# The next round's relative products in steps 0, 1, 2 and 4, and the maximum products spread anew

## The reference

```python
idx = jnp.arange(s)
dist = jnp.clip(idx[None, :] - idx[:, None], -R, R) + R
pe_k = rel_emb_k[dist]
pe_v = rel_emb_v[dist]
...
q = q / jnp.sqrt(jnp.asarray(hd, x.dtype))
score = jnp.einsum('bhqd,bhkd->bhqk', q, k) + jnp.einsum('bhqd,qkd->bhqk', q, pe_k)
attn = jax.nn.softmax(score, axis=-1)
ctx = jnp.einsum('bhqk,bhkd->bhqd', attn, v) + jnp.einsum('bhqk,qkd->bhqd', attn, pe_v)
...
x = x + _L0_attn_ref(_layernorm(x, axis=-1), ...)
x = x + _L0_ffn_ref(_layernorm(x, axis=-1), ...)
```

## Time and profile before

| | |
|---|---|
| median of 3 runs | 2382.93 us (2382.06 to 2384.38) |
| the profiled execution | 2382.3 us, span 2380.6 us |
| mean granted clock of TensorE | 0.981 of full |
| PE busy | 2282.5 us (96%) |
| DVE busy | 1906.6 us (80%) |
| ACT busy | 1429.9 us (60%) |
| POOL busy | 600.4 us (25%) |
| reduces of M, DVE line 1118 | 2048, mean 683 ns |
| exps, ACT line 1085 | 1792, mean 610 ns |

### The profile page before, as it was taken

One profiled execution on the slowest core, in us unless ns is written; L12 is line 12 of the kernel. 1 busy time (PEld: TensorE's weight loads), 2 busy tenths in 40 slices (PEclk: granted clock), 3 DMA queues, 4 the chain that ended last, 5 costly groups with the idle time before them and its releaser, 6 DMA issues. The chain is left out here.

```text
span 2380.6 us, 49031 instructions
## 1 busy us (share of the span) xinstructions
PE 2282.5 (96%) x19244; PEld 1182.6 (50%) x19244; DVE 1906.6 (80%) x3711; ACT 1429.9 (60%) x2720; POOL 600.4 (25%) x355
## 2 busy tenths in 40 slices
PE   7989999999999999999999999999999997999997
PEld 3515544444444444444444454444444444666665
DVE  6777888888888888888888888888888725999996
ACT  3406666666666666666666666666666673444442
POOL 5502222323322222222222222232332220111111
PEclk9959999999999999999999999999999998999999
DMA  5733533332333343433332333333222221111110
GB/s 157 199 88 91 138 85 93 94 95 83 92 92 92 97 110 96 108 99 96 92 93 84 99 98 85 92 97 92 83 83 84 76 77 43 45 44 44 47 50 20
DMA packets 275667, 210.43 MB, mean 88 GB/s; under 512 B 17058, under 2 KB 266628, under 8 KB 275332
## 3 DMA queue, kind: packets, MB, share of 16 engines
q1 hardware_dynamic: 274308, 203.37, 30.9%
q0 software_dynamic: 1152, 4.19, 0.6%
HBM read 113.35 MB, written 93.34 MB: 87 GB/s over the span
## 5 line engine op out<-in xcount | busy, mean ns | idle before, releaser
L1118 DVE TENSOR_REDUCE amax<-psA 128x1 f32<-128x512 f32 x2048 | 1300.5, 683 | 274.2 <-PE psA L828 270.1
L1085 ACT ACTIVATE probs<-psS 128x512 f32<-128x512 f32 x1792 | 927.3, 610 | 378.9 <-PE psS L936 378.9
L828 PE MATMUL psA<-keys,queries 96*128 96x512 bf16 x2048 | 772.0, 390 | 3.1 <-DVE amax L1118 1.9
L936 PE MATMUL psS<-queries,keys 102*128 102x512 bf16 (+7 forms) x2176 | 604.2, 342 | 0.1
L850 PE MATMUL psC<-probs,vals 128*32 128x512 f32 (+7 forms) x4352 | 475.0, 524 | 0.5 <-ACT probs L1085 0.5
L786 POOL TENSOR_TENSOR band_probs<-band_probs,side 128x2048 f32<-128x2048 f32 x64 | 288.9, 4534 | 515.6 <-PE psC L948 515.6
L828 PEld LDWEIGHTS psA<-keys,queries 96*128 96x128 bf16 x2048 | 195.3, 97 | 319.8 <-DVE amax L1118 179.3
L936 PEld LDWEIGHTS psS<-queries,keys 102*128 102x128 bf16 (+1 forms) x2176 | 205.9, 98 | 184.4 <-ACT rel_scores L1064 29.9
L1080 ACT ACTIVATE band_probs<-psS 128x512 f32<-128x512 f32 x256 | 153.0, 598 | 152.2 <-PE psS L925 152.0
L850 PEld LDWEIGHTS psC<-probs,vals 128*32 128x32 f32 (+1 forms) x4352 | 89.1, 102 | 193.8 <-ACT probs L1085 137.5
L1442 PE MATMUL psG<-w_gate_up_T,f_xqT 128*128 128x352 f32 x512 | 160.4, 467 | 0.9 <-ACT f_xqT L1496 0.9
(11 more groups left out here) (161 smaller groups left out, 2014.3 us busy)
## 6 DMA issues: line engine op xcount, KB each, us to landing
rel_skew<-rel_scores SPq DMA_DIRECT2D x32, 2048.0 KB, 7.5
rel_near<-rel_skew SPq DMA_DIRECT2D x64, 1024.0 KB, 8.2
keys<-k_ring SPq DMA_DIRECT2D x48, 256.0 KB, 5.8
queries<-q_parts SPq DMA_DIRECT2D x192, 64.0 KB, 2.4
ctx_d<-rden SPq DMA_DIRECT2D x32, 256.0 KB, 2.3
ctx_in<-ctx_d SPq DMA_DIRECT2D x32, 256.0 KB, 2.7
q_parts<-parts SPq DMA_DIRECT2D x16, 384.0 KB, 3.0
k_ring<-parts SPq DMA_DIRECT2D x12, 384.0 KB, 3.3
```

Source lines behind the costliest of these rows:

```text
L828: t.matmul(small("M", m, n), qs[0:NR, qb, h, u * P:(u + 1) * P], keys[0:NR, par, h, c0:c0 + NQ], start=True, stop=True).then_inc(small_rea ...
L936: ins = t.matmul(bank[:, o:o + k], keys[0:nr, par, h, c0:c0 + P], qs[0:nr, qb, h, q0:q0 + k], start=True, stop=True, skip_group_check=True)
L1085: ins = a.activation(probs[:, n % 4, half], src, ACT.Exp)
L1118: v.reduce_max(amax[:, pair, k:k + 1], small("M", m, n), AX.X).then_inc(small_taken, 1)
```

## The change

The four R of a round move from steps 4, 5, 6 and 7 to steps 0, 1, 2 and 4 (`RSTEPS`), with their copies on ACT, their `rel_maxima` on DVE (now behind the second M of the step after, not the third) and, through the last of them, SP's turn of `rel_scores`. The M of a round are spread anew: 9, 7, 6, 2, 4, 2, 3, 3, 3, 3, 5, 3, 4, 3, 4, 3 in steps 0 to 15 for 7, 7, 5, 3, 4, 3, 4, 3, 4, 4, 4, 4, 3, 3, 3, 3, and some stand at other places in their step. `AHEAD` becomes 10 for 9. The work is the same.

```diff
-RSTEP = 4
 RUNITS = APAIRS // 4
 SEQ = UNITS + RUNITS
+RSTEPS = (0, 1, 2, 4)
 
 PSTEP = 8
 
 ORDER = (
-    "SMSMVMSMSMMM", "SMSMMSMMSMMD", "SMSMVMMBSSM", "SMSSMSVM",
-    "SMSSMSMVRM", "SMSSMSVRM", "SMSSMSMVRM", "SMSSMSVRM",
-    "SMSSMSMVPM", "SMSSMSMVPM", "SMSSMSMVFPM", "SMSSMSMVPM",
-    "SMSSMSVFM", "SMSSMSVMT", "SMSSMSVM", "SMSSMSVM",
+    "SMSMVMMSMSMMRMM", "SMSMSMSMMRMDM", "SMSMVMMBSMSRM", "SMSSSVM",
+    "SMSSMSVMRM", "SMSSSVM", "SMSSMSVM", "SMSSMSVM",
+    "SMSSMSVPM", "SMSSMSVPM", "SMSSMSMVFMPM", "SMSSMSVPM",
+    "SMSMSSMVFM", "SMSSMSVMT", "SMSSMSMVM", "SMSSMSVM",
 )
@@
 def place(n, ends=False):
 
-    return n if ends else n + min(max(n // 2 - RSTEP, 0), RUNITS)
+    return n if ends else n + sum(r < n // 2 for r in RSTEPS)
 
 
 def rel_place(k):
 
-    return 2 * (RSTEP + k) + 2 + k
+    return 2 * RSTEPS[k] + 2 + k
@@
                         elif kind == "R":
                             if not ends:
-                                rel_products(it + 1, qb1, step - RSTEP)
+                                rel_products(it + 1, qb1, RSTEPS.index(step))
@@
-                    if n % 2 == 1 and RSTEP <= n // 2 < RSTEP + RUNITS and not ends:
-                        copy_rel(it + 1, n // 2 - RSTEP)
+                    if n % 2 == 1 and n // 2 in RSTEPS and not ends:
+                        copy_rel(it + 1, RSTEPS.index(n // 2))
@@
-                            if RSTEP < step <= RSTEP + RUNITS and k == 3 and not ends:
-                                rel_maxima(it + 1, step - RSTEP - 1)
+                            if step - 1 in RSTEPS and k == 2 and not ends:
+                                rel_maxima(it + 1, RSTEPS.index(step - 1))
```

## The result

The changed kernel takes 2388.76 us (median of 18 runs, 2386.59 to 2390.28) beside 2383.38 us for the kernel before on the same chips (18 runs). The ratio is 1.0021, interval 1.0015 to 1.0028: slower by 5.4 us, where 5.2 were forecast. The profiled execution has a span of 2387.0 us at a granted clock of 0.98, so it is 6.4 us longer than that of before.

The account below looks back on a forecast made before the run. PE was taken as the bound, streaming back to back with a few bank waits. The terms -8.4 - 2.7 + 13.0 + 2.9 + 0.4 gave +5.2 us, a forecast of 2388.0 us, range 2374 to 2397.

Parts of the forecast that it names:

- What bounds the kernel: PE streams back to back; a round is the sum of its products' start distances plus a few waits for banks.
- Removed: Step 8: PE's waits for psA banks held up by DVE go whole, saving 8.4 us.
- The block: Steps 0 to 2: waits at and around D become 0.52 us a round for 0.61, saving 2.7 us.
- The copies: Steps 3 and 5: S wait for psS banks that ACT's copies empty late, 0.42 us a round, +13.0 us.
- Tile switch: Step 10: P (64-column tiles) entered from an M costs 0.09 us more a round, +2.9 us.
- Prologue: Before the first turn_maxima: AHEAD 10 for 9 adds one reduce, 0.60 us, less 0.22 for an M saved later, +0.4 us.
- At no cost: POOL, SP's transfers, copy_context on ACT and the fourth M of step 14 add no time.
- Reduces at full length: Rival: DVE's queued reduces follow at full length, M9 to M17 wait 1.5 us for 0.52; 2416 us, chance 0.01.
- the S of steps 3 and 5 do not wait: Rival: psS is free when the last S of steps 3 and 5 arrives, the 13.0 us vanish; 2375 us, chance 0.13.
- DVE keeps pace: Rival: DVE keeps pace up to D in the block of steps 0 to 2, everything goes; 2360 us, chance 0.04.
- its queue is longer: Rival: DVE enters step 0 one reduce behind, waits up to M17 grow 0.3 us a round; 2397 us, chance 0.12.
- no change: Outcome class: a measured time of 2378.2 to 2387.7 us, within 0.2% (4.8 us); chance 0.40, against 0.41 for slower.

Follow-up runs that it names:

- kernel with R late: Kernel before with R kept in steps 4 to 7, M, D and rel_maxima placed anew so no product reaches its bank early: 2351.32 us, ratio 0.9867.

## Why the prediction was right, point by point

- *What bounds the kernel.* Right: the round is the sum of start distances and bank waits. Ten kernels followed from it within 3.3 us, from 2346 to 2403.
- *The total, 5.4 for 5.2.* That it came so close is in part luck: the interval is 3.1 us wide, and the stretch behind the last T alone scatters by 3.6 us from one execution to the next. What bears the prediction out are the waits, found one by one where it puts them.
- *Removed, 8.4 us.* Right in cause and size: no such wait is left after, and moving one rel_maxima in the kernel before gave 8 to 9 us. The place was misnamed: DVE is late in its step 8, PE waits in its step 9.
- *The block, 0.52 for 0.61.* Right in sum and nearly in place: 0.08, 0.24, 0.05 and 0.15 for 0.06, 0.24, 0.06 and 0.16.
- *The copies, 13.0 us.* Right: 0.07, 0.27 and 0.08 a round are the 0.42 that were forecast, and one M each moved ahead of the last S of steps 3 and 5 took back 8.3 to 9.4 us of them.
- *Tile switch.* 0.32 for 0.31, 3.1 us for 2.9: the upper bound was the value.
- *Prologue, 0.4 us.* Not shown by this pair: the first T starts at 173.6 us in both. But that start scatters: it lies between 173.0 and 173.7 in the three kernels with `AHEAD` 9 and between 173.4 and 174.1 in the six with 10, on average 0.4 later, where one reduce is 0.6.
- *At no cost.* Nothing of POOL, SP or the transfers appears among the waits of after. The gain on that side was zero too: rel_near lands earlier, and nobody asks for it.
- *Reduces at full length, 2416.* It did not come: the reduces of after overlap as those of before did, four in 2.47 us. The rule that the prediction set beside it, that the next op does not start until the pipe has emptied, is of the Trainium skill (VectorE: DVE Perf Modes, The DRAIN you can't avoid). The same section adds that a next op that is not held starts earlier, which the prediction left out, so the overlap does not speak against the section as a whole.
- *The rivals.* That the S of steps 3 and 5 do not wait, that DVE keeps pace, and that its queue is longer: none came. The sum of the terms as measured, -8.4 - 2.7 + 13.0 + 3.1 = +5.0 without the prologue, lies 0.4 under what was measured.
- The chances gave "no change" and "slower" almost the same, since the forecast lay on the bound; the result did too (its interval is 3.6 to 6.7 us).

## What to carry to other kernels

When an engine is busy all the time and the work stays the same, read distances between starts, not lengths: a wait is a distance longer than the same pair has elsewhere, and each can be priced by the moment its bank comes free. The step in which an engine is late need not be the one in which the other waits for it: here they were 8 and 9. What counts then is not on which step the work lies but what stands within two or three products of it; an R with two S ahead of it and too few M behind it cost 10 us (0.34 a round), and one M moved ahead of the last S took most of it back. Once the prices reproduce the kernel before to the hundredth, let them place the work: that gave 37 us (3 of them from a shorter prologue) where a plausible rearrangement lost 5.

## What the runs showed of the hardware that was not expected

- Entering a product with column tiles (32 or 64 wide) from a full one costs 0.09 to 0.10 us in TensorE (0.31 and 0.32 for 0.22), but not between two of them of the same width. In the kernel with R late, turn_back (32 wide) stands straight behind band_values (32 wide) and starts 1.77 us after it (first two lines). In the kernel before two M lie between (last three lines): the first starts 1.89 after band_values, and turn_back starts 0.31 after the second. So leaving the column tiles costs 0.12 more than staying in them, and an M put between the two takes 0.43 in place of 0.22.

```profile
1021.25 1.96 PE L949 MATMUL psC<-band_probs,vals 128*32 128x128 f32 x64
1023.02 1.06 PE L876 MATMUL psA<-ident,rden_cols 128*32 128x128 f32 x32
...
1035.48 1.95 PE L948 MATMUL psC<-band_probs,vals 128*32 128x128 f32 x64
1037.37 0.60 PE L828 MATMUL psA<-keys,queries 96*128 96x512 bf16 x2
1037.90 1.08 PE L875 MATMUL psA<-ident,rden_cols 128*32 128x128 f32 x32
```

- Relieving DVE of a whole reduce (0.6 us) ahead of a crowded lump freed 0.07 us at D. With three banks it was the spacing of the last four users that counted there; DVE sat idle just before.
